# Edge stage of a graph network kernel: the order of the first steps of its pipeline

## What is computed

```python
edge_index = stack([src, dst])                       # 25000 edges, sorted by dst
x = layernorm(x + L0(x, edge_index, node_vec))       # gated mean of neighbours, three products
x = layernorm(x + L1(x, edge_index, edge_weight))    # four attention heads
# a head of L1:
feats  = relu(x @ w1 + b1) @ w2 + b2                 # 256 -> 256 -> 64
hid    = relu(concat(feats[row], feats[col], elem) @ a1 + ab1)
e1     = leaky_relu(hid @ a2 + ab2); w = exp(e1 - max(e1))
pooled = segment_sum(w * feats[col], row) / (segment_sum(w, row) + 1e-10)
```

## Time and profile before

| | us |
|---|---|
| median of three runs | 3582.08 |
| the profiled execution | 3585.29 |
| its span in the trace | 3583.2 |
| PE busy / DVE / ACT / POOL | 3161.0 / 2730.8 / 1892.2 / 1802.4 |

### The profile page before, as it was taken

The page is one execution under the profiler, slowest core; times in us unless marked ns, Lnnn a source line. Parts: engine busy times, 40 slices in busy tenths (PEclk is TensorE's granted clock), DMA queues, the critical chain, the costliest instruction groups (busy, mean ns, idle before and its releaser), DMA issues. The chain is left out here.

```text
span 3583.2 us, 66785 instructions
## 1 busy us (share of the span) xinstructions
PE 3161.0 (88%) x15901; PEld 2177.7 (61%) x15901; DVE 2730.8 (76%) x9307; ACT 1892.2 (53%) x4499; POOL 1802.4 (50%) x1831
## 2 busy tenths in 40 slices
PE   4998887885898888499999999999999999995775
PEld 2455555553555555377777777777777777773333
DVE  4999997875333334388888888888888888887997
ACT  3666666663555545244444444444444444443886
POOL 0006675665777775544444444444444444420777
PEclk9999999997999999799999999999999999997998
DMA  4988777863555555433333333333333333322885
GB/s 146 322 312 274 259 259 266 276 214 123 184 170 177 177 183 183 136 124 117 117 117 117 117 116 115 116 115 116 115 115 116 116 116 116 116 80 78 270 270 196
DMA packets 289120, 596.12 MB, mean 166 GB/s; under 512 B 41438, under 2 KB 198922, under 8 KB 289062
## 3 DMA queue, kind: packets, MB, share of 16 engines
q1 hardware_dynamic: 212950, 362.51, 30.1%
q0 software_dynamic: 75744, 232.45, 20.0%
q10 hardware_dynamic: 368, 0.52, 0.0%
HBM read 287.39 MB, written 322.05 MB: 170 GB/s over the span
## 5 line engine op out<-in xcount | busy, mean ns | idle before, releaser
L1027 PE MATMUL bank<-w_node,xT 128*128 128x384 f32 x1564 | 605.5, 511 | 95.3 <-ACT bank L615 94.2
L1216 POOL TENSOR_TENSOR u_hc<-u_hc 128x1536 f32<-128x1536 f32 x98 | 270.2, 2758 | 759.5 <-DVE u_h L1326 735.4
L1438 PE MATMUL bank<-xh,w1h 128*128 128x512 f32 x1568 | 538.8, 425 | 19.1 <-DVE xl L1355 14.3
L1268 ACT ACTIVATE hidT<-bank,b1c 128x512 f32<-128x512 f32 x392 | 268.6, 685 | 536.3 <-PE bank L1438 536.2
L1438 PE MATMUL bank<-xh,w1l 128*128 128x512 f32 x1568 | 495.0, 397 | 0.0
L1438 PE MATMUL bank<-xl,w1h 128*128 128x512 f32 x1568 | 491.8, 395 | 0.0
L1349 DVE TENSOR_SCALAR hidT<-bank,b1c 128x512 f32<-128x512 f32 x392 | 294.3, 751 | 202.9 <-PE bank L1438 199.8
L1027 PEld LDWEIGHTS bank<-w_node,xT 128*128 128x128 f32 x1564 | 287.3, 198 | 264.8 <-ACT bank L615 118.8
L1452 PE MATMUL bank<-hidT,w2f 128*64 128x256 f32 x3136 | 381.7, 385 | 1.5 <-issue 1.5
L615 ACT ACTIVATE bank<-bias_all 128x512 f32<-128x512 f32 x391 | 235.0, 601 | 273.1 <-DVE H L725 267.8
L1364 DVE STREAM_TRANSPOSE feat<-catT 32x256 f32<-32x256 f32 x784 | 342.8, 437 | 17.1 <-ACT catT L1277 3.0
(11 more groups left out here) (273 smaller groups left out, 6612.9 us busy)
## 6 DMA issues: line engine op xcount, KB each, us to landing
hc_tab<-H SPq DMA_DIRECT2D x78, 960.0 KB
hc_tab<-zero_row SPq DMA_DIRECT2D x26, 2880.0 KB
er<-edge_tab SPq DMA_DIRECT2D x98, 512.0 KB, 4.4
X<-in_x SPq DMA_DIRECT2D x78, 640.0 KB
out_x<-O SPq DMA_DIRECT2D x78, 640.0 KB
edge_tab<-u_x SPq DMA_DIRECT2D x98, 256.0 KB, 2.2
edge_tab<-feat SPq DMA_DIRECT2D x98, 256.0 KB, 2.2
u_hc<-hc_tab,u_idx POOLq DMA_INDIRECT x392, 4.3
```

Source lines behind the costliest of these rows:

```text
L1027: ins = t_.matmul(p[:, 0:384], xT[i % XR][:, c * P:(c + 1) * P], w_node[:, c, :], start=False, stop=c == 1, skip_group_check=True)
L1216: g.tensor_tensor(c, c, u_hc[s][:, :, MULT:MULT + 3].unsqueeze(3).to_broadcast([P, 4, 3, P]), ALU.mult).then_inc(u_scaled, 1)
L1268: a.activation(hidT[m][:, :], bank[2 + m % 2][:, :], ACT.Relu, bias=b1c[:, m:m + 1])\
L1438: ins = t_.matmul(bank[2 + m % 2][:, :], w[:, c, m * P:(m + 1) * P], xx[s][:, c, :], start=n == 0, stop=n == 5)
```

## The change

Three reorderings in the steps that are written out, none in the loop, and no instruction added or removed.

- On POOL, `gate(0)` first calls `fetch(1)`; the later call of `fetch(1)` returns at once. The order becomes fetch(0), fetch(1), gate(0), gate(1), fetch(2), gate(2).
- On ACT, `root(1)` first calls `high(0)`: root(0), norm(0); high(0), root(1), norm(1); relu_0(0), root(2) and so on.
- On DVE, `stat(1)` first calls `low(0)`: stat(0), scale(0); low(0), stat(1), scale(1); stat(2), relu_1(0) and so on.

```diff
                 def fetch(u, s):
+                    if isinstance(u, int) and u == 1:
+                        if begun:
+                            return
+                        begun.append(u)
                     if after(u, 2):
+                begun = []
+
                 def gate(u, s):
+                    if isinstance(u, int) and u == 0:
+                        fetch(1, 1)
                     pool.wait_ge(u_in[s], (u - s) * 32 + 64)
                 def root(u, s):
+                    if isinstance(u, int) and u == 1:
+                        high(0, 0)
                     act.wait_ge(v_var, u + 1)
+                raised = []
+
                 def high(u, s):
+                    if isinstance(u, int) and u == 0:
+                        if raised:
+                            return
+                        raised.append(u)
                     act.wait_ge(t_ready, u + 1)
+                lowered = []
+
                 def stat(u, s):
+                    if isinstance(u, int) and u == 1:
+                        low(0, 0)
                     dve.wait_ge(u_gated, u + 1)
                 def low(u, s):
+                    if isinstance(u, int) and u == 0:
+                        if lowered:
+                            return
+                        lowered.append(u)
                     for c in range(2):
                         dve.wait_ge(t_high, u * 2 + (c + 1))
```

## The result

| | before | changed |
|---|---|---|
| median, us (19 runs each) | 3581.98 | 3576.57 |
| lowest to highest | 3578.41 to 3585.05 | 3572.01 to 3579.95 |
| ratio, 95% interval | | 0.9985 [0.9978, 0.9992] |
| span of the profiled execution | 3583.2 | 3574.2 |

The kernel is 5.4 us (0.15%) faster, between 2.9 and 7.9 us by the interval. Predicted were 7.1 us, 3575.0 in a range of 3572.7 to 3578.0.

What follows compares the result with a forecast made beforehand. PE bounds the edge stage once full; POOL's chain of waits up to gate(2) sets when that begins. Gate(2) 7.1 us earlier, the other moves nothing: 3582.08 - 7.1 = 3575.0 us, range 3572.7 to 3578.0.

Steps and rivals of the forecast that it cites:

- What sets the start: Ahead of the loop: gate(2) on POOL, through stat(2) and relu_1(0), sets hidden_3(0)'s start; both come 7.1 us earlier.
- Fetch(1) ahead of gate(0): On POOL: gate(0) starts 2.3 us later, but fetch(1)'s rows are hidden; gate(1) waits 1.5 us for stat(0)'s sum.
- The rows of fetch(2): POOL's wait ahead of gate(2): rows land 4.75 us after the last gather's start, between 4.45 and 5.19.
- The split: High(0) on ACT and low(0) on DVE, moved early: hidden_0(0) starts sooner, yet the two moves gain nothing by themselves.
- The slack: On DVE: stat(1)'s sum ends at 1473.9 at the latest, 1.9 us before gate(2) at 1476.0, so no cost.
- From there all keep their offsets: From hidden_3(0) on, POOL, DVE, ACT and PE keep order and offsets, so loop and last stage come 7.1 us earlier.
- the first rival: Steps 2 and 3: stalls shrink, up to 1.0 us, and full clock comes sooner; gain 8.2 to 9.4, chance 0.14.
- a sooner full clock: On PE: hidden_2(0) may run right ahead of hidden_3(0), reaching full clock sooner; worth up to 1.3 us.
- signs of being wrong: Trace signs against the forecast, among them hidden_3(0)'s distance to the end differing from before by more than 1 us.
- The sum of stat(1) meets fetch(2): Rival: DVE's sum overlaps the last gather, gate(2) 0.8 to 1.8 us later; gain 5.3 to 6.3, chance 0.17.
- Eight gathers: Rival on POOL: eight outstanding are too many, fetch(1) ends 3.5 us later; gain 2.7, 3579.4 us, chance 0.05.
- Median: Whole kernel: forecast 3575.0 us, 0.198% less; chance 0.59 for 3574.5 to 3576.0.

Runs made afterwards that it cites:

- a1: Changed kernel without the early high(0) and low(0), so only fetch(1) ahead of gate(0): 3841.8 us, ratio to the kernel before 0.9969.
- a2: Changed kernel without the early fetch(1), so only high(0) and low(0) moved: 3852.05 us, ratio to the kernel before 1.0008.
- a4: Changed kernel with 18 extra matmuls filling PE's pause ahead of hidden_3(0): hidden_3(0) to hidden_5(0) 3.70 us; no whole-kernel time given.
- a3: Changed kernel with step 0's u_x write held on SP until fetch(2)'s rows landed: gate(2) at 30.93 us into the stage; no whole-kernel time given.
- b3: Changed kernel with relu_1(0), relu_2(0), relu_3(0) moved ahead of norm work and fetch(2) ahead of gate(1): 3838.27 us, ratio to the kernel before 0.9978.
- b1: Changed kernel with relu_1(0) ahead of stat(2), relu_3(0) ahead of scale(2), relu_2(0) ahead of root(2): one execution, 3839.94 us.
- c1: The changed kernel run again unaltered, on another chip: 3844.42 us, ratio to the kernel before 0.9988.
- d2: Changed kernel with all relus PE waits for in steps 1 and 2 moved ahead of norm work: 3910.12 us, ratio to the kernel before 0.9969.
- d3: As d2, plus 18 extra matmuls ahead of turn(0) and 8 ahead of hidden_0(0) to keep PE busy: 3905.61 us, ratio to the kernel before 0.9967.
- c0: The kernel before run again unaltered, on the same chip as c1; the kernel before has a median of 3850.04 us there.
- d0: The kernel before run a third time, unaltered, on the same chip as d2: single execution 3925.28 us.
- d1: The changed kernel run a third time, unaltered, on the same chip as d2: single execution 3925.53 us.

## Why the prediction was right, and where it wasn't

- **What sets the start.** Right: gate(2), through stat(2) and relu_1(0). In the changed kernel, a1, a2 and a4 hidden_3(0) comes 8.48 to 8.51 us after gate(2) (predicted 8.50), and only the runs with fetch(1) ahead have an early gate(2).
- **Fetch(1) ahead of gate(0).** Predicted from the start of the stage (1444.83): gate(0) at 11.67, gate(1) at 17.41, the last gather of fetch(2) at 26.42. Measured: 11.62, 17.36, 26.34. The 0.30 us that a gate might have needed behind a gather were not needed.
- **The rows of fetch(2): the term that was mis-sized.** 5.94 us against 4.75 taken and 5.19 as the upper bound. I argued that the write of `u_x` at about 1468.7 would be nearly over. It was issued while gathers 2 to 4 were still being issued; held back in a3, the rows took 4.60. Nor does the slower figure belong to the write alone, as I had read it: fetch(3)'s rows took 5.39 us in the kernel before with none in flight. Gate(2) comes 6.0 to 6.6 us earlier in three pairs of traces, not 7.1.
- **The split.** Right: no gain that could be shown (a2) and none lost without it (a1). The slack too: `u_var` and `u_nb` were held by gate(1) as allowed for, stat(1)'s sum ended at 28.79 us (1472.13), 3.5 us ahead of gate(2), 3.3 if the 0.17 from sum to gate are taken off. I had 1.9, since low(0) was done at 27.7 and not at 27.9, and above all gate(2) came later.
- **"From there all keep their offsets".** Not quite. From hidden_3(0) to turn(6) the change gained another 0.2 to 2.4 us. On the first chip hidden_5(0) to hidden_0(3) took 42.56 us in place of 44.52, PE's stalls of 0.61, 0.58 and 0.39 us there being gone, and the 1.14 us more ahead of hidden_5(0), at half clock, take more than half of that back: 0.8 are left. This is the second part of the first rival. Its first part, a sooner full clock, did not come: hidden_2(0) was not next to hidden_3(0), and the time at half clock differs between executions of one kernel by 1.0 to 1.3 us. The span also ended 0.9 us sooner behind the stage (see the end). So the distance from hidden_3(0) to the end of the span fell from 2091.6 to 2090.1 us, and one of my signs of being wrong, more than 1 us there, did show.
- **The sum of stat(1) meets fetch(2).** It did not, but by little: 1470.92 lies behind the end of the last gather, 1470.63, by 0.3 us. `u_nb` was held, as I took it. Such a meeting is stat(2)'s sum with the first gather of fetch(3): that gather took 1.33 us in the changed kernel and 1.74 in b3, in place of 1.00.
- **Eight gathers.** They were issued at 0.95 to 1.00 us each. Nothing backed up.
- **Median.** 5.4 us, inside the range. The places on this chip say 6.8 for the loop: the last ACT operation of the edge stage is at 1805.83 (3249.17 - 1443.34) in place of 1812.65, 6.82 us earlier. The interval of the medians, 2.9 to 7.9, holds this. That 6.8 lies so near to 7.1 is luck in part: gate(2) brought 6.0, 1.1 less than predicted, and 0.8 came from stalls and clock that the sum had at nothing.

## What to carry to other kernels

In a prologue, list the waits of the engine that leads and what each waits for. Issuing the next gathers ahead of the first use turns a chain of waits for rows into one, at the price of the issue time. Moving work earlier gains only if the next engine's queue lets it through: here PE had three blocks ready early and sat behind one relu queued behind norm work, so the relu was the thing to move (in b1 hidden_3(0) comes 3.2 us earlier than in c1). Even that is not the whole: once PE is early it meets the next wait. Compare places inside the stage over several traces before a difference of 1 us is given a cause.

## What was not expected of the hardware

The rows of fetch(2) came in 4.60 us with no write about and in 5.3 to 6.1 us with one 256 KB write issued among its gathers (a3, one trace, against eight). That difference is larger than the one in the kernel before (4.45 against 5.19). With no write beside them, the last of 12 gathers in 26 us took 0.1 us more than the last of the first four on the same chip (4.50 in a2). Why fetch(3)'s rows took 5.4 to 5.6 us without a write in the kernel before and a2, and 4.58 in the first trace of the changed kernel, stays open.

TensorE ran at half clock after every idle time of 3.44 us or more in these steps (after the 4.18 us in the kernel before from the third matmul on). It kept full clock over idle times of 1.05 to 1.59 us (d2, d3), and after 2.17 us the clock had fallen (b1). How long it then stayed at half differed by 1.0 to 1.3 us between executions of one kernel, with the same instructions.

On the slower chips PE waited 0.3 to 0.5 us ahead of `features`, 17 to 27 times in 1600 us of the loop in groups a, b and c (6.4 and 9.3 us in c1 and c0), and in group d 42 to 47 times, up to 0.9 us each (25.5 to 29.7 us in d0, d1 and d2); on the first chip never. What differs there stays open. So does the 0.9 us by which the edge stage of the profiled execution ended earlier still (the last write and the barrier took 8.81 us before and 7.89 after). It is seen both ways in kernels with and without the change, 7.9 in a2 and 8.8 in b1, and is put down to no part of it.
